# Output product of the attention on high and low float16 parts: three float16 products instead of one float32 product

## The reference

```python
att = jnp.where(causal, att, jnp.finfo(att.dtype).min)
w = jax.nn.softmax(att, axis=-1)
y = jnp.einsum('bhts,bhsd->bhtd', w, v)
y = y.transpose(0, 2, 1, 3).reshape(Bx, Tx, H * D)
return y @ Wo          # (512, 1024) @ (1024, 128) per batch
```

## Time and profile before

| | us |
|---|---|
| median of 3 runs | 995.31 (992.98 to 999.05) |
| the profiled execution | 997.43 |
| its span | 995.7 |
| PE busy, whole span | 871.0 |
| PE weight loads busy | 640.5 |
| DVE busy | 672.0 |
| ACT busy | 630.5 |
| POOL busy | 675.7 |

### The profile page before, as it was taken

One profiled execution on the slowest core, in us unless ns is written; L12 is line 12 of the kernel. 1 busy time (PEld: TensorE's weight loads), 2 busy tenths in 40 slices (PEclk: granted clock), 3 DMA queues, 4 the chain that ended last, 5 costly groups with the idle time before them and its releaser, 6 DMA issues. The chain is left out here.

```text
span 995.7 us, 26021 instructions
## 1 busy us (share of the span) xinstructions
PE 871.0 (87%) x9516; PEld 640.5 (64%) x9516; DVE 672.0 (67%) x2475; ACT 630.5 (63%) x1190; POOL 675.7 (68%) x607
## 2 busy tenths in 40 slices
PE   4799999999999999999999998847788888886875
PEld 2367777777777777777777777634456556665542
DVE  7767878879878888988978976836433333333337
ACT  3678888888888888888888887722233333332305
POOL 7656665798698698699689689336265666664616
PEclk9899999999999999999999999977999999998988
DMA  5687787544335334444443350024333333331147
GB/s 160 170 272 240 237 223 214 136 122 123 84 102 135 92 93 124 104 103 106 108 118 92 91 135 29 17 81 128 101 102 100 95 100 105 111 101 52 38 164 264
DMA packets 95871, 123.76 MB, mean 124 GB/s; under 512 B 14478, under 2 KB 57053, under 8 KB 94848
## 3 DMA queue, kind: packets, MB, share of 16 engines
q1 hardware_dynamic: 87008, 106.69, 38.6%
q0 software_dynamic: 8736, 15.41, 4.9%
HBM read 32.96 MB, written 41.25 MB: 75 GB/s over the span
## 5 line engine op out<-in xcount | busy, mean ns | idle before, releaser
L2233 POOL TENSOR_TENSOR PL<-PF,PH 128x1280 f16<-128x1280 f32 x121 | 317.7, 2626 | 89.6 <-ACT PH L1572 87.7
L1798 DVE CUSTOM_DVE_ANT_0 JUNK<-PS,M 128x256 f16<-128x256 f32 (+3 forms) x512 | 224.3, 486 | 42.3 <-PE PS L1203 34.9
L1566 ACT ACTIVATE PF<-PS 128x512 f32<-128x512 f32 (+1 forms) x384 | 190.0, 522 | 71.8 <-PE PS L1236 62.3
L2275 POOL DMA_INDIRECT y_rows<-BIG,Q x145 | 140.8, 971 | 105.7 <-ACT BIG L1644 66.1
L1572 ACT ACTIVATE PH<-PF 128x1280 f16<-128x1280 f32 x128 | 162.4, 1269 | 4.4 <-PE PS L1255 2.2
L2266 POOL DMA_INDIRECT xe_rows<-PAY,DEST x128 | 128.6, 1005 | 41.9 <-issue 28.6
L1229 PE MATMUL PS<-Q,K 128*128 128x128 f16 (+3 forms) x512 | 152.7, 299 | 1.3 <-ACT PF L1566 1.1
L1253 PE MATMUL PS<-VH,PH 128*128 128x65 f16 x1280 | 137.9, 195 | 16.4 <-DVE Y L1838 12.0
L1254 PE MATMUL PS<-VL,PH 128*128 128x64 f16 x1280 | 138.1, 194 | 1.0 <-issue 1.0
L1255 PE MATMUL PS<-VH,PL 128*128 128x65 f16 x1280 | 138.1, 194 | 0.6 <-issue 0.6
L1253 PEld LDWEIGHTS PS<-VH,PH 128*128 128x128 f16 x1280 | 119.3, 98 | 25.4 <-issue 16.8
(11 more groups left out here) (265 smaller groups left out, 2121.8 us busy)
## 6 DMA issues: line engine op xcount, KB each, us to landing
K<-KH SPq DMA_DIRECT2D x128, 128.0 KB, 2.3
Q<-QH SPq DMA_DIRECT2D x128, 128.0 KB, 2.4
xe_rows<-PAY SPq DMA_DIRECT2D x20, 520.0 KB, 4.1
Q<-xe_rows SPq DMA_DIRECT2D x29, 325.0 KB
K<-KL SPq DMA_DIRECT2D x64, 128.0 KB, 2.3
Q<-QL SPq DMA_DIRECT2D x64, 128.0 KB, 2.4
y_rows<-PAY SPq DMA_DIRECT2D x16, 512.0 KB, 5.2
K<-in_L_ffn_w_dram SPq DMA_DIRECT2D x96, 64.0 KB
```

The lines of the kernel that those rows point to most:

```text
L1566: e.activation(PF[:, n % PBUF, c0:c0 + width], PS[:, k, 0:width], ACT.Exp).then_inc(s["c_exp"], 1)
L1798: e.tensor_tensor_reduce(JUNK[:, n_ttr % 2, 0:width], PS[:, base + ab, c0:c0 + width], M0[:, 512 - width:512], 1.0, -3e38, ALU.add, ALU.ma ...
L2233: e.tensor_tensor(PL[:, n % PBUF, :], PF[:, n % PBUF, :], PH[:, n % PBUF, :], ALU.subtract).then_inc(s["c_lp"], 1)
L2275: e.indirect_dma_start(out=y4[:, :], out_offset=bass.IndirectOffsetOnAxis(ap=XE[:, x_ % 6, k, 128:129].bitcast(I32), axis=0), in_=OUT[:, x ...
```

## The change

The output weights are split once, after loading, into WOH and WOL (float16); the float32 weights go into the staging tile for the null-value product, and the last two blocks also into WOE for the last unit. The y copy writes the float16 high part YTH; a new step "y low", one place later, has VectorE subtract it from PSUM into YTL. The product is made of three float16 matmuls where one float32 product stood. The last unit works in float32 as before. Also KP moves into the space of M0.

```diff
@@ unit_out
             step("y copy", u, pp)
             mark("yc", u, pp, by="c_am")
-            release(("yc", u, pp))
+            yield
+            step("y low", u, pp)
+            mark("yl", u, pp, by="c_dm")
+            release(("yc", u, pp), ("yl", u, pp))
             yield
@@ gate_products
         release(("wgt", 0))
         yield
+        step("split o")
+        mark("woh", 0, by="c_am")
+        mark("wol", 0, by="c_dm")
+        yield
@@ tensor, "out product"
-                w.wait_ge(l_wo, 16)
+                w.wait_ge(*at("woh", 0))
+                w.wait_ge(*at("wol", 0))
                 w.wait_ge(*at("yc", u, 1))
+                w.wait_ge(*at("yl", u, 1))
...
-                    e.matmul(o, YT[:, 0, t], WO[:, 2 * g, :], start=True, stop=False)
-                    i = e.matmul(o, YT[:, 1, t], WO[:, 2 * g + 1, :], start=False, stop=(g < 3))
+                    for pp in range(2):
+                        e.matmul(o, YTH[:, pp, t], WOH[:, 2 * g + pp, :], start=(pp == 0), stop=False)
+                        e.matmul(o, YTH[:, pp, t], WOL[:, 2 * g + pp, :], start=False, stop=False)
+                        i = e.matmul(o, YTL[:, pp, t], WOH[:, 2 * g + pp, :], start=False, stop=(pp == 1 and g < 3))
@@ scalar
-                e.activation(YT[:, pp, :], MISC, ACT.Copy).then_inc(s["c_am"], 1)
+                w.wait_ge(*at("ul", 0))
+                e.activation(YTH[:, pp, :], MISC, ACT.Copy).then_inc(s["c_am"], 1)
+            elif name == "split o":
+                w.wait_ge(l_wo, 32)
+                e.activation(WOH[:, :, :], WO, ACT.Copy).then_inc(s["c_am"], 1)
@@ vector
+            elif name == "y low":
+                u, pp = a
+                w.wait_ge(*at("yc", u, pp))
+                w.wait_ge(*at("wo", u - 1))
+                e.tensor_tensor(YTL[:, pp, :], MISC, YTH[:, pp, :], ALU.subtract).then_inc(s["c_dm"], 1)
+            elif name == "split o":
+                w.wait_ge(l_wo, 32)
+                w.wait_ge(*at("woh", 0))
+                e.tensor_tensor(WOL[:, :, :], WO, WOH[:, :, :], ALU.subtract).then_inc(s["c_dm"], 1)
```

More of the change, by code:

```diff
@@ L843, in program @@
     BIG = sb("BIG", [128, 2816], F32)
-    YT = BIG[:, 0:1024].rearrange("p (a n) -> p a n", a=2)
+    YTH = BIG[:, 0:512].bitcast(F16).rearrange("p (a n) -> p a n", a=2)
+    YTL = BIG[:, 512:1024].bitcast(F16).rearrange("p (a n) -> p a n", a=2)
+    YT = BIG[:, 1024:2048].rearrange("p (a n) -> p a n", a=2)
     RT = sb("RT", [128, 512], F32)
@@ L853, in program @@
     UL = sb("UL", [128, 16], F16)
-    WO = sb("WO", [128, 8, 128], F32)
+    WOH = sb("WOH", [128, 8, 128], F16)
+    WOL = sb("WOL", [128, 8, 128], F16)
+    WOE = sb("WOE", [128, 2, 128], F32)
     NVO = sb("NVO", [128, 128], F32)
@@ L917, in program @@
     KW = sb("KW", [128, NT, 4], F32)
-    KP = sb("KP", [128, ND, NT, 4], F32)
     GW = sb("GW", [128, ND, NT], F32)
+    KP = M0[:, 0:ND * NT * 4].rearrange("p (d n k) -> p d n k", d=ND, n=NT)
     PS = ctx.enter_context(nc.psum_tensor("PS", [128, 8, 512], F32))
@@ L970, in program @@
     wq_f, wk_f, wv_f = STG[:, 0:1024], STG[:, 1024:2048], STG[:, 2048:3072]
+    WO = STG[:, 3072:4096].rearrange("p (k n) -> p k n", k=8)
     wqs, wqT = BIG[:, 0:1024], BIG[:, 1024:2048]
@@ L1302, in tensor @@
                     t = slice(q * 128, (q + 1) * 128)
-                    i = e.matmul(PS[:, 5, t], YT[:, 0, t], WO[:, 6, :], start=True, stop=True)
+                    i = e.matmul(PS[:, 5, t], YT[:, 0, t], WOE[:, 0, :], start=True, stop=True)
                 i.then_inc(s["c_pm"], 1)
@@ L1321, in tensor @@
                     o, t = PS[:, 6 - half, q * 128:(q + 1) * 128], slice(q * 128, (q + 1) * 128)
-                    e.matmul(o, YT[:, 1, t], WO[:, 7, :], start=True, stop=False)
+                    e.matmul(o, YT[:, 1, t], WOE[:, 1, :], start=True, stop=False)
                     i = e.matmul(o, RT[:, t], NVO[:, :], start=False, stop=True)
@@ L1603, in scalar @@
                 w.wait_ge(*at("wgt", 0))
+                w.wait_ge(*at("wol", 0))
+                w.wait_ge(*at("nvo", 0))
                 for q in range(*span(*half)):
@@ L2335, in sync @@
                 e.dma_start(wv_f, Wv).then_inc(l_wv, 16)
-                e.dma_start(WO[:, :, :], Wo.rearrange("(k p) n -> p k n", p=128)).then_inc(l_wo, 16)
+                e.dma_start(WO, Wo.rearrange("(k p) n -> p k n", p=128)).then_inc(l_wo, 16)
+                e.dma_start(WOE[:, :, :], Wo[768:1024, :].rearrange("(k p) n -> p k n", p=128)).then_inc(l_wo, 16)
                 e.dma_start(WGS[:, :], wg).then_inc(l_wg, 16)
```

## The result

The changed kernel takes 1084.3 us (median of 4, 1081.23 to 1092.26) against 995.02 for the kernel before on the same chip: a ratio of 1.094, 95% interval 1.089 to 1.098. The forecast was 1025, with a range up to 1046. The sign was right, the size three times too small: +89 us, not +30.

What follows compares the result with a forecast made beforehand. TensorE was taken to bound the attention stage, VectorE and ScalarE close behind. Losses of 34 us in six batches, 3.5 outside and 1.7 for the split made +39, cut to +30: 1025 us, range 992 to 1046.

Steps and rivals of the forecast that it cites:

- What bounds the kernel: Attention stage, 100 to 600 us: TensorE leads, busy 488 of 500 us, with ScalarE 425 and VectorE 422 close behind.
- TensorE's part: Output product: 24 float16 matmuls replace 8 float32 products, 1.78 to 1.34 us a unit, 13.6 us saved over 31 units.
- the 2.6 us of contention in the upper bound: Split of the output weights on VectorE: could stand behind one GpSimd low-half subtraction, adding 2.6 us; included in the +42 bound.
- Prices of ScalarE's and VectorE's instructions: Attention stage: ScalarE's y copy stays 0.60 us; 62 VectorE subtractions of 0.69 us, 0.60 start to start, 37 us in all.
- What the new instruction stands in front of: VectorE's queue: the low half waits for ScalarE's copy and delays everything behind it, 5.6 us a batch, 34 in six.
- The replay: One batch of four units re-timed from the trace: losses 0.8, 3.3, 0.3, 1.2 us; +39 us in all with the split.
- I take three quarters: Whole sum: ScalarE catches up while TensorE stands and waits shrink, so +39 us becomes +30.
- replay in full or more: Rival: VectorE's lateness passes into the third unit, or the clock falls to 0.97, about 15 us; 1034 us and above, chance 0.20.
- The time is TensorE's: Rival: low halves are hidden and only the shorter product counts, -12 us, 983 us; chance 0.11.
- loss and saving about cancel: Rival: ScalarE's y copy comes early in a slower rhythm, only VectorE's excess work is paid, 1000 us; chance 0.14.
- The skill's rule: VectorE instructions with two SBUF inputs contend with GpSimd reading SBUF, single-input ones do not; the 62 subtractions stay untouched.
- What would show it: Changed profile: values matmuls wait for Y, VectorE idles before low halves, 24 matmuls of 0.056 us, VectorE's share near 85%.

Runs made afterwards that it cites:

- e2: Changed kernel without the low half of Y: float16 product alone, third matmul reads the high half again; ratio 0.998 to the kernel before.
- e6: Kernel before with 62 more VectorE instructions of about 0.6 us where the low halves would stand, waiting for nothing; ratio 1.003.
- e13: Changed kernel with four VectorE routing steps (DROP, MS, gate sum, cast IFA) moved out of GpSimd's way in six batches; ratio 1.054.
- e10: Kernel before with GpSimd's low p subtraction cut to 4 of 1280 columns from the third head on; ratio 1.011.
- e11: Changed kernel with GpSimd's low p subtraction cut to 4 of 1280 columns, as in e10; ratio 1.055 to the kernel before.
- e18: e15 with the gate sum and the cast IFA moved, in six batches, to behind the second low half; ratio 1.017 to the kernel before.
- e17: e13 with each low half cut to 4 of 512 columns and the low parts of Y left out; ratio 1.036 to the kernel before.
- e3: Changed kernel, order and waits kept, low half subtracting only 4 of 512 columns, third matmul reading the high half; ratio 1.057 to the kernel before.
- e1: Kernel before with one more yield ahead of the release in unit_out, giving the changed kernel's order of all other steps; ratio 1.030.
- e8: Changed kernel without the extra place in the order, low half laid out at the place of ScalarE's copy; ratio 1.102 to the kernel before.
- e15: Changed kernel without the extra place in the order, MS directly behind DROP, each low half in a VectorE gap; ratio 1.031.

## Why the prediction was right and wrong

**What bounds the kernel: right.** TensorE led, and lateness of VectorE and ScalarE was what counted.

**TensorE's part: right as busy time, half as gain.** Kernel after, unit 17's product, the first and the last of twelve of its 24 matmuls:

```profile
453.01 0.23 PE L1297 MATMUL PS<-WOH,BIG 128*128 128x128 f16 x1
...
453.64 0.22 PE L1299 MATMUL PS<-WOH,BIG 128*128 128x128 f16 x1
```

Eleven steps in 0.63 us are 0.057 each, as taken. Alone (e2) they took 13.3 us off TensorE's busy time, for 13.6 foreseen, and 6.4 us off the stretch. The split took 1.23 us, not 1.7, with no low p beside it; the 2.6 us of contention in the upper bound did not come, and unit 0 turns 0.2 us later (70.21 for 70.01).

**Prices of ScalarE's and VectorE's instructions: right** (0.596 and 0.691 us), and that the work is hidden in VectorE's idle time holds for the work alone (e6).

**What the new instruction stands in front of: this mechanism right, its price wrong, a second one missed.** The replay had VectorE waiting 2.25 us for the first copy of the second unit (395.08 to 397.33); it waited 2.13. What comes next is wrong: "DROP at 397.93, Y at 398.40", which keeps for DROP the 0.47 us that it took in the earlier trace rows. Pushed back, it met low p and took 1.68 us to the next start. That is the step that failed: a duration carried over to a place where another engine holds the instruction. The same again in "D to Y another 1.0": the cast in it took 2.24 us. The values matmuls of unit 17 came 3.6 us later than before after the unit's turn (5.32 against 1.74 us), not 2.3, the next ones 8.4 us later, not 3.3, and the unit lost 10.8 us. The hint was in the quoted row: DROP's 0.54 us at 395.08 in the earlier trace rows is itself a short hold-up, three times the 0.19 it takes when free (e13). It ends at 395.62, 0.05 behind a low p of the kernel before:

```profile
392.93 2.64 POOL L2233 TENSOR_TENSOR PL<-PF,PH 128x1280 f16<-128x1280 f32 x1
```

Where the blocking is gone, the replay's terms fare better: in e13 the four units lose 2.3, 4.0, 0.7 and 1.6 us, 8.6 a batch, where 0.8, 3.3, 0.3 and 1.2 were forecast, 5.6. Between e10 and e11, where low p is cut on both sides, they are 1.3, 4.2, 0.7 and 0.8, 6.9 a batch, and 48 us over the stretch for the replay's 39: the replay in full is near, its three quarters are not.

**"I take three quarters": wrong.** Nothing was recovered. Instead the clock fell around TensorE's waits, so that its own late work got longer: the opposite sign, and a term that the sum had at nothing. The clock stood in the rival "replay in full or more" at 0.97 and 15 us; it was 0.95 over the stretch, with 64.9 us at half speed, of which TensorE was busy nearly all (9.21 of 10.2 us in the two pieces of unit 17 above). Half of 64.9 is 32 us. The rows of the stretch say the same: against e2, with as many matmuls and no time at 1.2 GHz, TensorE is busy 33.4 us more (572.3 for 538.8), against e18 30.5. So the +92.9 us are 13.3 us less for the shorter product, 33.4 more for the same matmuls at the lower clock, and 72.8 more of standing (91.8 for 19.0).

**The rivals.** "The time is TensorE's" and "loss and saving about cancel" fell. "Replay in full or more" (1034 us and above, chance 0.20) is where the time came out, with the clock in it; but the range ended at 1046, and neither it nor this rival had the blocking.

**The skill's rule** was weighed only against the added instructions, and there it held: the low halves, with a PSUM input, were not touched. It should have been put to every instruction that the change displaces.

**What would show it:** of the four signs three came (waits for line 1869, VectorE idle before the low half, matmuls of 0.056 us). VectorE's busy share fell to 80% (402 of 500 us) instead of staying at 85%: everyone waited.

Taken off in this order, the +93 us are: 36 for DROP, the cast and the clock that goes with them (e13), 21 for the low halves' work where it follows a wait (e17 against e13), and 36 for the waits and the shifted order, DF's hold-up among them. Another order gives other shares: with the work taken off first (e3), it is worth 47. Open is how the last 36 divide, since e1 (+22) and e8 (the shift taken out, 12 worse) contradict a sum; open too is which falls of the clock a given wait causes, for no run changed the clock alone.

## What to carry to other kernels

When a change makes an engine late, list what moves behind it and what it will now overlap with. A narrow instruction with two SBUF inputs, or a cast between SBUF tiles, that costs 0.2 us can cost 2 when it slides into a long GpSimd operation on SBUF. Ask then whether TensorE soon needs what stands behind it: if not, it costs nothing; if so, moving one cast can be worth more than the change. And where the change adds waits of TensorE, look at the granted clock around them: here it added 33 us.

## What the runs showed of the hardware

- GpSimd's 2.6 us subtraction holds VectorE instructions with two SBUF inputs to its end: DROP for 1.75 us, MS 1.85, DF 1.20, MM up to 2.33 (e18), and also a cast of 128x16 with one input, 2.24 to 2.52. Instructions with a PSUM input (0.69), a reduction of one SBUF tile (0.28) and a reciprocal of one (0.18) pass beside it at their usual time.
- TensorE's granted clock fell to 1.2 GHz in unit 17 while TensorE stood in a 3.41 us wait, for 6.8 us, though it was busy again from 445.63 on; and once more for 3.4 us, 2.3 us after a wait of 2.24 us. The length of a wait alone did not decide it in these runs: e1 has six waits of 1.72 us, and behind four of them the clock fell for 3.4 us each, e11 six of 1.84 between 100 and 600 us and none there. In e15 three of the six waits of 2.27 us have a stretch at 1.2 GHz beside them, and three have not.
- The same 8001 matmuls of the stretch kept TensorE busy 538.8 us with no time at 1.2 GHz (e2) and 572.3 us with 64.9 us of it (the changed kernel).
